# Setup of a fused four-layer graph network: edge lists loaded in other row groups and taken in another order, x in four pieces on two queues

## The chip, the core and the metric

The kernel runs on one core of one Trainium2 chip. The time is that of one execution on the device, in microseconds (us); smaller is better. A core has five engines with queues of their own: PE (TensorE, matrix products), DVE (VectorE), ACT (ScalarE), POOL (GpSimd) and SP (SyncE, which here only issues transfers). They meet through semaphores. The core's 16 DMA engines move the data.

## The reference

Four graph layers on 6,250 nodes with 128 features, 100,000 edges sorted by target, each followed by a residual sum and a layer norm:

```
x = norm(x + segsum((x @ W)[src] * (edge_attr @ edge_w), dst) + b)
x = norm(x + relu(segsum((x @ W_r)[src, edge_type] * edge_weight, dst) + bias))
x = norm(x + gcn(x, edge weights from a small MLP on x[src], x[dst]) + b)
x = norm(x + gin(x)): 4 times  h = x + segsum(x[src], dst); x = relu(h @ W1 + b1) @ W2 + b2
```

Inputs that matter here: `x` (6250 x 128, f32) and four lists of 100,000 words: `src`, `dst`, `edge_type` (integers) and `edge_weight` (f32).

## The kernel before, in words

Nodes are padded to 49 blocks of 128 (NB), handled as 7 chunks (NCH) of 7 blocks (CB). Edges are handled in 98 groups (NG) of 1024 (GE); 97 groups are full (FULL), the last holds 672 (TAIL). Each group is 8 sets (TPG) of 128 edges.

The setup, which the change rewrites, does four things side by side.

1. **Loads.** `load_list` reads a list into a tile `raw` of 98 partitions (one group in each) in two transfers: columns 0 to 671 of 98 partitions, and columns 672 to 1023 of 97 partitions. SP loads x blocks 0 to 20, dst, src, x blocks 21 to 47, and the last 106 rows of x; ACT loads W0, the types, the weights, then eight copies of `edge_w`. The second transfer of each list waits for DVE's fills (`s_fill`).
2. **Chunks.** For each chunk, `setup_turn` transposes 7 blocks of x on PE, ACT copies them out of PSUM, `setup_products` multiplies them by W0, ACT copies the product, and SP stores it to the table `xw_rows`. Before chunks 0 to 3 PE runs `turn_list`, which transposes one list each into PSUM, from where DVE takes it (`take_list`) as `srci`, `dstf`, `reli`, `wedge`.
3. **Keys and plan.** DVE waits for all eight list transfers (`s_load`), then makes three keys of each edge (`keyraw`, stored to `key_rows`) and `lists16`, then finds each group's smallest and largest target. PE turns these rows (`turn_plan`), and DVE derives `basei` and `nwini`: the plan. All engines read `nwini` (`window_count`).
4. **Histogram.** DVE marks the edges' target tiles in four wide instructions, PE sums them in two sets of 49 matmuls, and DVE forms running sums (`starts`), by which the key blocks are fetched (`c_start`).

Then comes round 0: for each of the 98 groups POOL issues 8 indirect gathers of 128 rows from `xw_rows` (line 767), PE multiplies edge attributes by `edge_w`, DVE multiplies the two (the messages, line 2091), and PE sums by target. Beside it DVE, PE and ACT build blocks of a dense matrix from the keys. POOL may run 5 groups (AHEAD) in front of the messages: the line is `pool.wait_ge(s_msg[(g - AHEAD) % 2], (g - AHEAD) // 2 + 2)`. Rounds 1 and 2 gather in the same way; the last layer uses the dense matrix. Every engine runs its instructions in program order.

On DVE `link` makes an instruction signal a semaphore and the next one wait for it. `raw` and the scratch rows `ka`, `kb` lie in `XT2`, where the gathers land, so POOL waits for `c_keys` before the first gather.

Of the kernel before, what the change touches and what calls it, by code (L numbers as in the profile page):

```python
# [6 lines left out]
I32 = mybir.dt.int32  # L7
# [34 lines left out]
def gnn_program(nc, x, src, dst, edge_attr, edge_type, edge_weight, W0, edge_w, b0, W1r, bias1,  # L42
# [28 lines left out]
    with ExitStack() as ctx:  # L71
# [205 lines left out]
        a_ready = sem2("a_ready")  # L277
        a_done = sem2("a_done")
# [22 lines left out]
        m_gath = sem2("m_gath")  # L301
        r_land = [sem(f"r_land{k}") for k in range(NS)]
# [218 lines left out]
        def _(sp):  # L521
            def x_blocks(lo, hi):
                return x[lo * P:hi * P, :].rearrange("(b p) f -> p b f", p=P)
            half = (NCH // 2) * CB
            sp.dma_start(blocks(X[:, 0:half * P]), x_blocks(0, half)).then_inc(s_xload, 16)
            for r, a in ((RDST, dst), (RSRC, src)):
                load_list(sp, r, a)
            sp.dma_start(blocks(X[:, half * P:(NB - 1) * P]), x_blocks(half, NB - 1)).then_inc(s_xload2, 16)
            sp.dma_start(X[0:LASTROWS, (NB - 1) * P:NPAD], x[(NB - 1) * P:N, :]).then_inc(s_xload2, 16)

# [71 lines left out]
            sp.wait_ge(c_list, 48)  # L602
# [142 lines left out]
        def _(pool):  # L745
            pool.iota(iota[:, :], [[1, NPAD]], base=0, channel_multiplier=0,
# [3 lines left out]
            pool.memset(acc[:, :], 0.0).then_inc(s_zero, 1)  # L750
# [21 lines left out]
            pool.wait_ge(c_keys, 1)  # L772
# [103 lines left out]
        def _(act):  # L876
            act.dma_start(W0s[:, :], W0[:, :]).then_inc(s_wload, 16)
            for r, a in ((RTYP, edge_type), (RWGT, edge_weight)):
                load_list(act, r, a)
            for j in range(TPG):  # L880
                act.dma_start(EWb[j * EDIM:(j + 1) * EDIM, j, :], edge_w[:, :]).then_inc(c_tail, 16)
# [25 lines left out]
            setup_store(NCH - 1)  # L907
            for o, i in loads:
# [390 lines left out]
        def _(pe):  # L1299
# [3 lines left out]
            def turn_list(r):  # L1303
                pe.wait_ge(s_prep, r + 1)
                if r >= 1:
                    pe.wait_ge(s_pe, r)
                v = raw[r].rearrange("g (p j) -> g j p", j=TPG)
                for j in range(TPG):
                    m = pe.transpose(ps4[:, j * P:j * P + NG], v[0:NG, j, :], ident[0:NG, 0:NG])
                m.then_inc(s_pt, 1)  # L1310

            def setup_turn(c):
                if c == 0:
                    pe.wait_ge(s_xload, 16)
                elif (c + 1) * CB > NCH // 2 * CB:
                    pe.wait_ge(s_xload2, 32)
# [17 lines left out]
            def turn_plan():  # L1334
                pe.wait_ge(s_prep, 5)
# [12 lines left out]
            pe.wait_ge(s_plan, 1)  # L1348
# [478 lines left out]
        def _(dve):  # L1827
# [8 lines left out]

            for r in (RDST, RSRC, RTYP, RWGT):
                if r == RDST:
                    dve.memset(raw[r][0:NG, TAIL:GE].bitcast(I32), -1)
                else:  # L1840
                    dve.memset(raw[r][0:NG, TAIL:GE], 0.0)
            dve.memset(X[:, (NB - 1) * P:NPAD], 0.0)
            dve.memset(EWb[:, :, :], 0.0).then_inc(s_fill, 1)
# [17 lines left out]
            dve.wait_ge(s_iota, 2)  # L1861
# [3 lines left out]
            dve.tensor_scalar(ident[:, :], iota[:, 0:P], pcol[:, 0:1], None, ALU.is_equal).then_inc(s_ident, 1)  # L1865

            dve.tensor_copy(iotaS[:, :], iota[:, 0:KS * P])
            dve.tensor_copy(iotaB[:, :], iota[:, 1:BN + 1])
            dve.wait_ge(s_ident, 1)
            dve.tensor_copy(identh[:, :], ident[:, :]).then_inc(s_ident, 1)  # L1870
            link(dve.tensor_reduce(fold[:, :], ident[:, :].rearrange("p (j c) -> p c j", c=HB), AXX, ALU.add))
            link(dve.tensor_reduce(blockof[:, :], ident[:, :].rearrange("p (j c) -> p j c", c=HB), AXX, ALU.add))


            dve.wait_ge(s_load, 16 * 8)
            lists = ((RSRC, srci), (RDST, dstf), (RTYP, reli), (RWGT, wedge))
            srcn, dstn = raw[RSRC][0:NG, :].bitcast(I32), raw[RDST][0:NG, :].bitcast(I32)
            shift_s, shift_t = (KS * P).bit_length() - 1, TB.bit_length() - 1
            link(dve.tensor_scalar(ka.bitcast(I32), srcn, KS * P - 1, None, ALU.bitwise_and))
            link(dve.tensor_copy(keyraw[:, :, 0], ka.bitcast(I32)))  # L1880
            link(dve.tensor_scalar(ka.bitcast(I32), srcn, shift_s - shift_t, 15 * TB, ALU.logical_shift_right, ALU.bitwise_and))
            link(dve.tensor_copy(kb.bitcast(I32), srcn))
            link(dve.tensor_copy(raw[RSRC][0:NG, :], srcn))
            dve.sem_inc(s_prep, 1)
            link(dve.tensor_scalar(kb.bitcast(I32), kb.bitcast(I32), P - 1, None, ALU.bitwise_and))
            link(dve.tensor_copy(lists16.rearrange("g (j p) -> g p j", p=P), kb.bitcast(I32).rearrange("g (p j) -> g p j", j=TPG)))
            link(dve.tensor_scalar(kb.bitcast(I32), dstn, TB - 1, None, ALU.bitwise_and))
            link(dve.scalar_tensor_tensor(keyraw[:, :, 1], ka.bitcast(I32), 1.0, kb.bitcast(I32), ALU.add, ALU.add))
            link(dve.tensor_scalar(ka.bitcast(I32), dstn, shift_t, None, ALU.logical_shift_right))
            link(dve.tensor_copy(keyraw[:, :, 2], ka.bitcast(I32)))  # L1890
            link(dve.tensor_copy(raw[RDST][0:NG, :], dstn))
            dve.sem_inc(s_prep, 1)

            def take_list(r):
                dve.wait_ge(s_pt, r + 1)
# [3 lines left out]

            take_list(RSRC)  # L1900
            link(dve.tensor_copy(raw[RTYP][0:NG, :], raw[RTYP][0:NG, :].bitcast(I32)))
            link(dve.scalar_tensor_tensor(raw[RTYP][0:NG, :], raw[RSRC][0:NG, :], float(RELS), raw[RTYP][0:NG, :],
                                          ALU.mult, ALU.add))
            dve.sem_inc(s_prep, 2)


            link(dve.tensor_scalar(ka, raw[RDST][0:NG, :], 0.0, float(NPAD), ALU.is_lt, ALU.mult))
            link(dve.tensor_tensor(ka, ka, raw[RDST][0:NG, :], ALU.add))
            link(dve.tensor_reduce(small[0:NG, 0:1], ka, AXX, ALU.min))
            link(dve.tensor_reduce(small[0:NG, 1:2], raw[RDST][0:NG, :], AXX, ALU.max))  # L1910
            take_list(RDST)
            link(dve.tensor_tensor(kb[:, 0:GE - P], raw[RDST][0:NG, 0:GE - P], ka[:, P:GE], ALU.is_equal))
            link(dve.tensor_reduce(small[0:NG, 2:3], kb[:, 0:GE - P], AXX, ALU.max))
# [4 lines left out]
            take_list(RTYP)  # L1918
            take_list(RWGT)

            dve.wait_ge(s_pt, 5)
# [16 lines left out]
            dve.sem_inc(c_keys, 1)  # L1938
            dve.sem_inc(s_plan, 1)
            nwin, more = window_count(dve)  # L1940

# [221 lines left out]
            dve.wait_ge(c_list, 48)  # L2163
# [434 lines left out]
```

## Time and profile before

| | us |
|---|---|
| median of 3 runs (4726.57 to 4737.44) | 4734.65 |
| the profiled execution's own time | 4725.84 |
| its span, first to last instruction | 4723.9 |
| POOL busy in the span | 2448.5 |
| PE busy in the span | 3383.4 |
| DVE busy in the span | 2343.9 |

The profile is of one execution. Its span lies 1.94 us below that execution's time, and that execution 8.8 us below the median of the runs. Line numbers in the rows are those of the kernel before. In a row `128x1024 f32` is partitions by elements; `[0.76 <-DVE big L2091]` is idle time before the instruction and what ended it. SPq, ACTq and DVEq are instructions of an engine's queue that are not counted as work, such as issuing a transfer or reading a value.

### The profile page before, as it was taken

Reading aid. Unit: us, or ns where it says so; the run is one execution under the profiler, and the core shown is the slowest. Engines: PE = TensorE matmul, PEld = TensorE weight load, DVE = VectorE, ACT = ScalarE, POOL = GpSimd, SP = SyncE. Lnnn points to the kernel's source line nnn. Section 1 sums busy time; section 2 is a strip of 40 time slices with the busy share of each in tenths; the row PEclk is TensorE's granted clock in tenths of the full one; section 3 lists DMA queues with packets and bytes.
Section 4 is the critical chain, followed back from the end, with each engine's and each line's share of the span. In section 5 each row is a group of like instructions: output and inputs, shape, how many; then the busy total and the mean of one; then the engine's idle time right before and its main releaser. Section 6 shows DMA issues by size and latency. Waiting matters only on the chain.

```text
span 4723.9 us, 66594 instructions
## 1 busy us (share of the span) xinstructions
PE 3383.4 (72%) x22549; PEld 2232.3 (47%) x22549; DVE 2343.9 (50%) x5563; ACT 1316.7 (28%) x3113; POOL 2448.5 (52%) x2489
## 2 busy tenths in 40 slices
PE   3888888886667777674333333337888999999998
PEld 3554555553445455443222222227884555555554
DVE  6755555553565556554555555556883111111122
ACT  1232322332122222222444444445882000000000
POOL 3777777774777777775777777772330000000000
PEclk8999999998888888886555555557999999999999
DMA  3334344442333333333777777777876777777776
GB/s 106 104 118 124 122 134 130 129 124 96 92 96 98 100 103 101 99 92 95 199 199 197 198 200 200 196 198 257 301 283 257 286 288 280 279 275 278 287 293 226
DMA packets 506525, 855.10 MB, mean 181 GB/s; under 512 B 111339, under 2 KB 284439, under 8 KB 506180
## 3 DMA queue, kind: packets, MB, share of 16 engines
q1 hardware_dynamic: 338752, 542.03, 32.6%
q0 software_dynamic: 87808, 179.98, 15.1%
q10 hardware_dynamic: 79620, 128.70, 7.6%
q8 instruction: 190, 3.11, 0.3%
q14 instruction: 155, 1.27, 0.1%
HBM read 632.93 MB, written 217.55 MB: 180 GB/s over the span
## 4 chain that ended last, share of the span: by engine, by line
POOL 48%; PE 30%; issue 16%; DVE 3%; DMA 1%; ACT 1%; SPq 0%; DVEq 0%; POOLq 0%; ACTq 0%
POOL big L767 32%; POOL big L794 16%; PE psS L1775 11%; PE psA L1775 11%; PE psS L1451 4%; PE psA L1655 1%; PE ps L1721 1%; PE ps L1712 1%; ACT big L1143 1%; DVE xsb L1956 1%; DMA big<-in_src_dram 0%; PE ps L1644 0%; DMA big<-A_rows 0%; PE ps L1386 0%; PE psS L1356 0%
## 5 line engine op out<-in xcount | busy, mean ns | idle before, releaser
L767 POOL DMA_INDIRECT big<-ht_rows,reli x784 | 788.4, 1006 | 276.7 <-issue 238.6
L767 POOL DMA_INDIRECT big<-xw_rows,srci x784 | 766.9, 978 | 309.5 <-issue 238.3
L794 POOL DMA_INDIRECT big<-axt_rows,srci x784 | 746.1, 952 | 264.8 <-issue 238.5
L1451 PE MATMUL psS<-big 128*128 128x128 f32 x3136 | 506.8, 329 | 311.3 <-DMA big<-ht_rows,reli 310.1
L1451 PEld LDWEIGHTS psS<-big 128*128 128x128 f32 x3136 | 475.5, 240 | 381.8 <-DMA big<-ht_rows,reli 347.6
L851 POOL TENSOR_TENSOR xsb<-xsb,l3b2r 128x896 f32<-128x896 f32 x6 | 12.5, 2079 | 1114.9 <-DMA xsb<-x_keep 1114.9
L1775 PE MATMUL psS<-big,xsb 128*128 128x448 f16 x1372 | 485.3, 354 | 17.6 <-ACT xsb L1198 15.0
L1596 PE MATMUL ps<-identh,xsb 128*128 128x128 bf16 x784 | 101.4, 311 | 549.0 <-DVE xsb L2267 549.0
L1775 PE MATMUL psA<-big,xsb 128*128 128x448 f16 x1372 | 485.1, 354 | 0.0
L1775 PE MATMUL psS<-big,acc 128*128 128x448 f16 x1372 | 483.8, 353 | 0.0
L1775 PE MATMUL psA<-big,acc 128*128 128x448 f16 x1372 | 483.8, 353 | 0.0
L929 ACT CAST xsb<-ps 128x416 f16<-128x416 f32 x392 | 197.8, 505 | 759.1 <-PE ps L1499 759.1
L1499 PE MATMUL ps<-xsb 128*128 128x416 bf16 x1960 | 401.5, 363 | 0.0
L1486 PE MATMUL psA<-xsb 128*128 128x416 bf16 x1960 | 363.1, 339 | 0.0
L1596 PEld LDWEIGHTS ps<-identh,xsb 128*128 128x128 bf16 x784 | 75.5, 141 | 577.2 <-DVE xsb L2267 577.2
L1523 PE MATMUL ps<-xsb,attrT 128*128 128x512 f32 x392 | 212.6, 669 | 127.7 <-DVE big L2091 127.3
L2033 DVE TENSOR_SCALAR xsb<-iotaS,keys 128x512 bf16<-128x512 f16 x980 | 285.2, 356 | 34.2 <-PE ps L1499 21.7
L2091 DVE TENSOR_TENSOR big<-big,ps 128x1024 f32<-128x1024 f32 x98 | 119.5, 1219 | 363.7 <-DMA big<-xw_rows,srci 363.6
L929 ACT CAST xsb<-psA 128x416 f16<-128x416 f32 x392 | 198.1, 505 | 356.8 <-PE psA L1486 356.1
L1499 PEld LDWEIGHTS ps<-xsb 128*128 128x128 bf16 x1960 | 199.4, 105 | 160.2 <-issue 39.9
L1999 DVE TENSOR_TENSOR big<-big,dstf 128x1024 f32<-128x1024 f32 x196 | 240.0, 1224 | 57.4 <-issue 36.4
L2036 DVE TENSOR_SCALAR xsb<-iotaB,kk 128x416 bf16<-128x416 f16 x980 | 263.4, 331 | 0.0
(291 smaller groups left out, 5074.1 us busy)
## 6 DMA issues: line engine op xcount, KB each, us to landing
big<-A_rows SPq DMA_DIRECT2D x112, 2744.0 KB, 13.4
A_rows<-xsb ACTq DMA_DIRECT2D x196, 416.0 KB, 2.6
xg_rows<-big SPq DMA_DIRECT2D x98, 512.0 KB, 3.8
big<-xg_rows SPq DMA_DIRECT2D x98, 512.0 KB, 4.1
marks_rows<-big SPq DMA_DIRECT2D x98, 354.0 KB
big<-marks_rows SPq DMA_DIRECT2D x98, 354.0 KB, 5.5
big<-srcq_list SPq DMA_DIRECT2D x98, 256.0 KB
ht_rows<-big ACTq DMA_DIRECT2D x28, 512.0 KB
```

Source lines behind the costliest of these rows:

```text
L767: pool.indirect_dma_start(ring[g % len(ring)][:, j * D:(j + 1) * D], None, table[:, :], bass.IndirectOffsetOnAxis(ap=lists[:, g * TPG + j: ...
L794: pool.indirect_dma_start(wide[g % NS][:, j, :], None, axt_rows[:, :], bass.IndirectOffsetOnAxis(ap=srci[:, g * TPG + j:g * TPG + j + 1], ...
L929: act.copy(Astage[:, u, :, k, :], bank(k).rearrange("p (s n) -> p s n", n=TB)).then_inc(b_ev, 1)
L1451: m = pe.matmul(psS[b][:, 0:P], rows[b][:, j * P:(j + 1) * P], marks[b][:, j * P:(j + 1) * P], start=(j == 0), stop=(j == TPG - 1))
L1486: mm = pe.matmul(bank(k), ohS[:, u, (j * KS + k) * P:(j * KS + k + 1) * P], ohB[:, u, j * BN:(j + 1) * BN], start=(j == 0), stop=(j == BT ...
L1499: mm = pe.matmul(bank(k), ohS[:, u, (j * KS + k) * P:(j * KS + k + 1) * P], ohB[:, u, j * BN:(j + 1) * BN], start=(j == 0), stop=(j == BT ...
L1523: m = pe.matmul(ps4[:, h * 512:(h + 1) * 512], attrT[:, b, :], EWb[:, 4 * h:4 * h + 4, :].rearrange("p j f -> p (j f)"), start=True, stop= ...
L1596: m = pe.transpose(turned(b)[:, j * P:(j + 1) * P], ohN[:, b, j * P:(j + 1) * P], identh[:, :])
L1775: m = pe.matmul(sums, parts_of(l, t // CB)[:, t % CB, k, :], Aring[:, r, :, t, :], start=(t == 0), stop=(t == NB - 1))
L1999: return dve.tensor_tensor(tiles(onehot[:, b, :]), iota[:, window(base, w)].unsqueeze(1).broadcast_to([P, TPG, P]), columns(dstf, it, b), ...
L2033: dve.tensor_scalar(ohS[:, u, j * KS * P:(j + 1) * KS * P], iotaS[:, :], keys[:, u, j, 0:1], None, ALU.is_equal)
L2036: last = dve.tensor_scalar(ohB[:, u, j * BN:(j + 1) * BN], iotaB[:, :], kk[:, u, j:j + 1], None, ALU.is_equal)
```

## The change

- Each list is loaded as 96 whole rows of 1024, then 2 rows of 672, then the 352 words that are left of row 96. src and dst have semaphores of their own (those of `a_ready`, whose later wait count is raised by 48).
- x is loaded in pieces of 1, 2, 2 and 2 chunks. SP issues piece 0, src, dst, and piece 2; ACT issues W0, piece 1, types, weights, piece 3 and the last 106 rows. The eight `edge_w` transfers come after the chunks.
- `raw`, `ka`, `kb` lie in `acc`; the float copies of src and dst (`srcf`, `dstc`) lie in `xsb`. POOL no longer waits for `c_keys`. ACT zeroes `acc` after the lists have been taken, where POOL did it at the start.
- POOL writes the first 128 columns of `iota` and `pcol`, and the other 6144 columns after DVE has made `ident`.
- DVE handles src and dst first, then the plan, then the types, the keys, the last two lists, and `iotaS` and `iotaB`.
- PE turns src behind the products of chunk 0, dst behind chunk 2, the plan's rows behind chunk 3, types and weights behind chunk 6.
- `key_rows` is stored as 96 rows, 1 row and 1 short row, before as 98 and 97 rows.

The diff, cut to its core:

```diff
-        raw = [XT2[:, k * GE:(k + 1) * GE] for k in range(4)]
+        raw = [acc[:, k * GE:(k + 1) * GE] for k in range(4)]
-        ka, kb = (XT2[0:NG, k * GE:(k + 1) * GE] for k in (4, 5))
+        ka, kb = (acc[0:NG, k * GE:(k + 1) * GE] for k in (4, 5))
+        srcf, dstc = (xsb[0:NG, k * GE:(k + 1) * GE] for k in range(2))
+        PIECES = ((0, 1), (1, 3), (3, 5), (5, NCH))
...
+        WHOLE = FULL - 1
+        def load_rows(eng, r, a, done):
+            v = raw[r] if r == RWGT else raw[r].bitcast(I32)
+            eng.dma_start(v[0:WHOLE, :], a[0:WHOLE * GE].rearrange("(g e) -> g e", e=GE)).then_inc(done, 16)
+            eng.dma_start(v[WHOLE:NG, 0:TAIL], bass.AP(tensor=a.tensor, offset=WHOLE * GE, ap=[[GE, NG - WHOLE], [1, TAIL]])
+                          ).then_inc(done, 16)
+        def load_rest(eng, r, a, done):
+            v = raw[r] if r == RWGT else raw[r].bitcast(I32)
+            eng.dma_start(v[WHOLE:FULL, TAIL:GE], as_row(a[WHOLE * GE + TAIL:FULL * GE])).then_inc(done, 16)
+        def load_x(eng, k):
+            lo, hi = PIECES[k][0] * CB, min(PIECES[k][1] * CB, NB - 1)
+            eng.dma_start(blocks(X[:, lo * P:hi * P]), x[lo * P:hi * P, :].rearrange("(b p) f -> p b f", p=P)
+                          ).then_inc(x_in[k], 16)
...
+            load_x(sp, 0)
+            load_rows(sp, RSRC, src, s_lsrc)
+            load_rows(sp, RDST, dst, s_ldst)
+            sp.wait_ge(s_fill, 1)
+            load_rest(sp, RSRC, src, s_lsrc)
+            load_rest(sp, RDST, dst, s_ldst)
+            load_x(sp, 2)
...
             pool.wait_ge(s_plan, 1)
-            pool.wait_ge(c_keys, 1)
...
             act.dma_start(W0s[:, :], W0[:, :]).then_inc(s_wload, 16)
+            load_x(act, 1)
             for r, a in ((RTYP, edge_type), (RWGT, edge_weight)):
-                load_list(act, r, a)
-            for j in range(TPG):
-                act.dma_start(EWb[j * EDIM:(j + 1) * EDIM, j, :], edge_w[:, :]).then_inc(c_tail, 16)
+                load_rows(act, r, a, s_load)
+            load_x(act, 3)
+            act.wait_ge(s_fill, 1)
+            act.dma_start(X[0:LASTROWS, (NB - 1) * P:NPAD], x[(NB - 1) * P:N, :]).then_inc(x_in[3], 16)
+            for r, a in ((RTYP, edge_type), (RWGT, edge_weight)):
+                load_rest(act, r, a, s_load)
...
+            act.wait_ge(s_iota, 3)
+            act.wait_ge(s_pe, 4)
+            act.activation(acc[:, :], iota[:, :], ACT.Copy, scale=0.0).then_inc(s_zero, 1)
...
             for c in range(NCH):
-                if c < 4:
-                    turn_list(c)
-                elif c == 4:
-                    turn_plan()
                 if c + 1 < NCH:
                     setup_turn(c + 1)
                 setup_products(c)
+                if c == 0:
+                    turn_list(RSRC)
+                elif c == 2:
+                    turn_list(RDST)
+                elif c == 3:
+                    turn_plan()
+            turn_list(RTYP)
+            turn_list(RWGT)
```

How the order moves on two engines. On PE, the first matmuls of the setup before (`psA<-ident,big` are `setup_turn`, `ps<-ident,big` a list, `ps<-W0s` the products):

```order
L1320 MATMUL psA<-ident,big 128x128 x7
L1309 MATMUL ps<-ident,big 128x98 x8
L1320 MATMUL psA<-ident,big 128x128 x7
L1330 MATMUL ps<-W0s,xTs 128x128 x7
L1309 MATMUL ps<-ident,big 128x98 x8
L1320 MATMUL psA<-ident,big 128x128 x7
L1330 MATMUL ps<-W0s,xn 128x128 x7
```

and of the change, where the lists lie in `xsb` (src, dst) and `acc`:

```order
L1349 MATMUL psA<-ident,big 128x128 x14
L1359 MATMUL ps<-W0s,xTs 128x128 x7
L1339 MATMUL ps<-ident,xsb 128x98 x8
L1349 MATMUL psA<-ident,big 128x128 x7
L1359 MATMUL ps<-W0s,xn 128x128 x7
L1349 MATMUL psA<-ident,big 128x128 x7
L1359 MATMUL ps<-W0s,xTs 128x128 x7
L1339 MATMUL ps<-ident,xsb 128x98 x8
```

The first list now stands behind two turned chunks and the first products; the plan's three rows stand behind chunk 3 here, and stood behind all four lists before.

On DVE, from the last step on a list's smallest and largest values to the plan, before:

```order
L1915 TENSOR_REDUCE small<-big 98x1
L1916 TENSOR_TENSOR small<-small 98x1
L1896 CAST reli<-ps 128x8x98
L1896 COPY wedge<-ps 128x8x98
L1923 COPY rowf<-psS 1x98
L1924 TENSOR_TENSOR rowf<-psS,rowf 1x98
```

and, in the change, from the end of the plan to the histogram's first instruction (types, keys, `lists16`, two lists taken, `iotaS`, `iotaB`):

```order
L1954 CAST acc<-acc 98x1024
L1955 SCALAR_TENSOR_TENSOR acc<-xsb,acc 98x1024
L1957 TENSOR_SCALAR acc<-acc 98x1024
L1958 CAST big<-acc 98x1024
L1959 TENSOR_SCALAR acc<-acc 98x1024
L1960 TENSOR_SCALAR acc<-acc 98x1024
L1961 SCALAR_TENSOR_TENSOR big<-acc 98x1024
L1962 TENSOR_SCALAR acc<-acc 98x1024
L1963 CAST big<-acc 98x1024
L1964 TENSOR_SCALAR acc<-acc 98x1024
L1965 CAST xsb<-acc 98x128x8
L1915 CAST reli<-ps 128x8x98
```

The first of the change's rows comes right behind DVE's reading of `nwini`; behind the last stand `wedge`, `iotaS` and `iotaB`, then the copy into `psS` with which the histogram begins (line 1946 before). Before, all this work but the histogram stood ahead of the plan.

## Rows read from the trace of the kernel before

**Rows 1.** Page, part 5, the gathers of the first round (line 767)

```profile
L767 POOL DMA_INDIRECT big<-xw_rows,srci x784 | 766.9, 978 | 309.5 <-issue 238.3
```

**Rows 2.** Waits of POOL: total us, times, longest us

```profile
POOL big L767 <- DMA xw_rows<-big: 70.4, 1, 70.4
...
POOL big L767 <- DVE big L2091: 0.8, 1, 0.8
```

**Rows 3.** Chain that ended last, first 140 us: start, us, what

```profile
12.03 22.27 DMA big<-in_src_dram
34.39 0.70 DVE big L1879
...
45.49 0.70 DVE big L1891
...
67.34 0.26 DVE rowf L1923
...
73.42 0.19 DVE psS L1946
...
123.76 2.90 issue
...
131.37 1.14 DVE big L2091
...
132.76 1.68 POOL big L767
```

**Rows 4.** Timeline of SP's and ACT's queues: start us, us, issue

```profile
9.59 15.40 ACTq L881 DMA_DIRECT2D xsb<-in_L_gnn_edge_w_dram  x8
...
24.31 11.76 SPq L529 DMA_DIRECT2D big<-in_x_dram  x1
25.33 1.28 ACT L889 ACT_TABLE_LOAD   x1 [25.33 <-issue]
26.63 0.91 ACT L889 COPY xTs<-psA 128x896 f32<-128x896 f32 x1
```

**Rows 5.** Windows: each engine's busy us, PEclk, DMA share, GB/s

```profile
4.00:8.00 4.00, 0.00 (x0) 0.00 (x0) 2.73 (x17) 0.00 (x0) 4.00 (x3) 1.00 1.05 291
15.00:20.00 5.00, 0.00 (x0) 0.00 (x0) 0.00 (x0) 0.00 (x0) 0.00 (x0) 1.00 0.07 25
```

**Rows 6.** Timeline of TensorE, setup matmuls at the slow and fast rate

```profile
56.82 1.55 PE L1309 MATMUL ps<-ident,big 98*128 98x98 f32 x8 [3.82 <-DVEq L1898]
...
58.16 1.70 PE L1320 MATMUL psA<-ident,big 128*128 128x128 f32 x7
...
59.66 2.82 PE L1330 MATMUL ps<-W0s,xTs 128*128 128x128 f32 x14
...
68.14 1.80 PE L1330 MATMUL ps<-W0s,xTs 128*128 128x128 f32 x14
...
71.02 1.80 PE L1330 MATMUL ps<-W0s,xn 128*128 128x128 f32 x14 [0.32 <-ACT big L895]
```

**Rows 7.** Timeline of DVE in the setup, one memset of POOL

```profile
6.23 5.31 POOL L750 MEMSET acc<- 128x6272 f32 x1
...
6.55 5.35 DVE L1867 CAST iotaS<-big 128x512 f16<-128x512 f32 x1
...
11.82 0.36 DVE L1868 CAST iotaB<-big 128x416 f16<-128x416 f32 x1
...
46.33 1.56 DVE L1896 CAST srci<-ps 128x784 int32<-128x784 f32 x1 [0.15 <-DVE big L1891]
...
48.45 0.69 DVE L1901 CAST big<-big 98x1024 f32<-98x1024 int32 x1 [0.56 <-DVE srci L1896]
...
50.56 0.69 DVE L1907 TENSOR_SCALAR big<-big 98x1024 f32<-98x1024 f32 x1 [0.16 <-DVE big L1902]
```

**Rows 8.** Timeline, the first gather, then DVE's markings in the loop

```profile
81.93 1.14 POOL L767 DMA_INDIRECT big<-xw_rows,srci  x1 [70.39 <-DMA xw_rows<-big]
...
128.75 1.40 DVE L2033 TENSOR_SCALAR xsb<-iotaS,keys 128x512 bf16<-128x512 f16 x5
```

More of the change, by code:

```diff
@@ L277, in gnn_program @@
         a_ready = sem2("a_ready")
+        s_lsrc, s_ldst = a_ready
+        LISTED = 16 * 3
         a_done = sem2("a_done")
@@ L301, in gnn_program @@
         m_gath = sem2("m_gath")
+        x_in = [s_xload, *m_gath, s_xload2]
+        PIECED = 16
         r_land = [sem(f"r_land{k}") for k in range(NS)]
@@ L521, in _ @@
         def _(sp):
[L522 to L529, printed above, removed]
+            load_x(sp, 0)
[5 more added lines that the diff above has]
+            load_x(sp, 2)
             def rows_of(table, c):
@@ L745, in _ @@
         def _(pool):
-            pool.iota(iota[:, :], [[1, NPAD]], base=0, channel_multiplier=0,
+            pool.iota(iota[:, 0:P], [[1, P]], base=0, channel_multiplier=0,
                       allow_small_or_imprecise_dtypes=True).then_inc(s_iota, 1)
@@ L749, in _ @@
                       allow_small_or_imprecise_dtypes=True).then_inc(s_iota, 1)
-            pool.memset(acc[:, :], 0.0).then_inc(s_zero, 1)
+            pool.wait_ge(s_ident, 1)
+            pool.iota(iota[:, P:], [[1, NPAD - P]], base=P, channel_multiplier=0,
+                      allow_small_or_imprecise_dtypes=True).then_inc(s_iota, 1)
             def gathers(it, idx_ready, gathered, table):
@@ L907, in _ @@
             setup_store(NCH - 1)
+            act.wait_ge(s_fill, 2)
+            for j in range(TPG):
+                act.dma_start(EWb[j * EDIM:(j + 1) * EDIM, j, :], edge_w[:, :]).then_inc(c_tail, 16)
             for o, i in loads:
@@ L1312, in setup_turn @@
             def setup_turn(c):
[L1313 to L1316, printed above, removed]
+                for k, (lo, hi) in enumerate(PIECES):
+                    if c == lo:
+                        pe.wait_ge(x_in[k], 2 * PIECED if hi == NCH else PIECED)
                 if c:
@@ L1834, in link @@
                 dve.wait_ge(s_chain, chain[0])
+            dve.wait_ge(s_iota, 2)
+            dve.tensor_scalar(ident[:, :], iota[:, 0:P], pcol[:, 0:1], None, ALU.is_equal).then_inc(s_ident, 1)
             for r in (RDST, RSRC, RTYP, RWGT):
                 if r == RDST:
-                    dve.memset(raw[r][0:NG, TAIL:GE].bitcast(I32), -1)
+                    dve.memset(raw[r][WHOLE:NG, TAIL:GE].bitcast(I32), -1)
                 else:
-                    dve.memset(raw[r][0:NG, TAIL:GE], 0.0)
-            dve.memset(X[:, (NB - 1) * P:NPAD], 0.0)
-            dve.memset(EWb[:, :, :], 0.0).then_inc(s_fill, 1)
+                    dve.memset(raw[r][WHOLE:NG, TAIL:GE], 0.0)
+            dve.memset(X[:, (NB - 1) * P:NPAD], 0.0).then_inc(s_fill, 1)
+            dve.wait_ge(s_ident, 1)
+            dve.tensor_copy(identh[:, :], ident[:, :]).then_inc(s_ident, 1)
+            link(dve.tensor_reduce(fold[:, :], ident[:, :].rearrange("p (j c) -> p c j", c=HB), AXX, ALU.add))
+            link(dve.tensor_reduce(blockof[:, :], ident[:, :].rearrange("p (j c) -> p j c", c=HB), AXX, ALU.add))
+            dve.memset(EWb[:, :, :], 0.0)
             dve.memset(attr[:, :, :], 0.0)
@@ L1864, in _ @@
             dve.memset(invs[:, 0, 1:2], 1.0 / (FIRST * LOW))
[L1865 to L1871, printed above, removed]
@@ L1887, in _ @@
[L1887 to L1891, printed above, removed]
+            dve.wait_ge(s_lsrc, LISTED)
+            link(dve.tensor_copy(srcf, srcn))
@@ L1898, in take_list @@
                 dve.sem_inc(s_pe, 1)
-            take_list(RSRC)
[L1901 to L1913, printed above, removed]
+            link(dve.tensor_scalar(ka, dstc, 0.0, float(NPAD), ALU.is_lt, ALU.mult))
+            link(dve.tensor_tensor(ka, ka, dstc, ALU.add))
+            link(dve.tensor_reduce(small[0:NG, 0:1], ka, AXX, ALU.min))
+            link(dve.tensor_reduce(small[0:NG, 1:2], dstc, AXX, ALU.max))
+            link(dve.tensor_tensor(kb[:, 0:GE - P], dstc[:, 0:GE - P], ka[:, P:GE], ALU.is_equal))
+            link(dve.tensor_reduce(small[0:NG, 2:3], kb[:, 0:GE - P], AXX, ALU.max))
+            take_list(RSRC)
             link(dve.tensor_tensor(kb[:, 0:GE - 1], ka[:, 0:GE - 1], ka[:, 1:GE], ALU.is_gt))
@@ L1917, in _ @@
             dve.sem_inc(s_prep, 1)
-            take_list(RTYP)
-            take_list(RWGT)
-            dve.wait_ge(s_pt, 5)
+            take_list(RDST)
+            dve.wait_ge(s_pt, 3)
             lo, hi, span, base = (rowf[:, k, :] for k in range(4))
@@ L1937, in _ @@
             link(dve.tensor_copy(nwini[:, :], hi[:, 2:4]))
-            dve.sem_inc(c_keys, 1)
             dve.sem_inc(s_plan, 1)
             nwin, more = window_count(dve)
+            shift_s, shift_t = (KS * P).bit_length() - 1, TB.bit_length() - 1
+            dve.wait_ge(s_load, 16 * 6)
+            link(dve.tensor_copy(raw[RTYP][0:NG, :], raw[RTYP][0:NG, :].bitcast(I32)))
+            link(dve.scalar_tensor_tensor(raw[RTYP][0:NG, :], srcf, float(RELS), raw[RTYP][0:NG, :], ALU.mult, ALU.add))
+            dve.sem_inc(s_prep, 2)
+            link(dve.tensor_scalar(ka.bitcast(I32), srcn, KS * P - 1, None, ALU.bitwise_and))
+            link(dve.tensor_copy(keyraw[:, :, 0], ka.bitcast(I32)))
+            link(dve.tensor_scalar(ka.bitcast(I32), srcn, shift_s - shift_t, 15 * TB, ALU.logical_shift_right, ALU.bitwise_and))
+            link(dve.tensor_scalar(kb.bitcast(I32), dstn, TB - 1, None, ALU.bitwise_and))
+            link(dve.scalar_tensor_tensor(keyraw[:, :, 1], ka.bitcast(I32), 1.0, kb.bitcast(I32), ALU.add, ALU.add))
+            link(dve.tensor_scalar(ka.bitcast(I32), dstn, shift_t, None, ALU.logical_shift_right))
+            link(dve.tensor_copy(keyraw[:, :, 2], ka.bitcast(I32)))
+            link(dve.tensor_scalar(kb.bitcast(I32), srcn, P - 1, None, ALU.bitwise_and))
+            link(dve.tensor_copy(lists16.rearrange("g (j p) -> g p j", p=P), kb.bitcast(I32).rearrange("g (p j) -> g p j", j=TPG)))
+            dve.sem_inc(c_keys, 1)
+            take_list(RTYP)
+            take_list(RWGT)
+            dve.wait_ge(s_iota, 3)
+            dve.tensor_copy(iotaS[:, :], iota[:, 0:KS * P])
+            dve.tensor_copy(iotaB[:, :], iota[:, 1:BN + 1])
             HSH = HB.bit_length() - 1
```

38 lines of the change are left out of this document (13 added, 25 removed).

## The prediction

> **What bounds the kernel now.** I read the page first, then POOL's waits, the chain that ended last over the first 140 us, and the timelines of each engine there. In the page the 784 gathers of round 0 are 767 us of POOL work plus 310 us of idle time between them, most of it issue [rows 1]: POOL paces that round, so what moves POOL's steady stream moves all that follows. POOL's stream could begin when the table `xw_rows` is stored; it waited 70.4 us for it [rows 2] and began at 81.93 [rows 8]. But it may run only 5 groups, 40 gathers, in front of DVE's messages. The 41st gather began at 132.76 [rows 3], and POOL had waited 0.8 us for DVE's first message [rows 2], which ran at 131.37. So at this place the two sides are nearly level: an earlier first gather alone gives at most 0.8 us, and an earlier DVE gives nothing unless the first gather moves too. The change moves both.
>
> The chain of waits says what sets DVE: src lands at 34.30 (12.03 + 22.27), DVE starts on the keys at 34.39, reaches the plan at 67.34, the histogram at 73.42 and the loop after 123.76 [rows 3]. From 73.42 on nothing is edited on DVE, and I carry that stretch over as it is. The question is thus: at which time does DVE begin the histogram?
>
> The loads explain the 34.30. From 4 to 8 us the DMA engines moved 291 GB/s; from 15 to 20 us they moved 25 GB/s at a share of 0.07, about one engine of 16 [rows 5]. Meanwhile the queues stood: ACT was busy until 24.99 issuing eight small transfers, and SP until 36.07 with the last issue of x [rows 4]. I read the 25 GB/s as the 97-row transfers, 97 rows of 1408 bytes each: four of them are 0.546 MB, and at 25 GB/s 21.9 us, which fits the gap.
>
> **The change part by part.** *Loads.* Now the bulk is 96 whole rows a list. x is 3.2 MB, the lists 1.6 MB, W0 0.07 MB: 4.87 MB at 291 GB/s are 16.7 us, from about 2 us on, so all has landed by about 19 us. src and dst stand ahead of half of x on SP; with the two queues taking turns they land near 12 us. I estimate that ACT's last issue ends at 17.5 us: a transfer's issue seems to end a little ahead of the data before it. Bounds: 12 us if ACT's queue gets the larger share, 19 us if the smaller. The last 106 rows of x still go as a transfer of their own, in that ACT queue.
> By the Trainium skill ("DMA: Bandwidth & Descriptors", section on why a DMA increments its semaphore by 16) a transfer uses the largest number of engines up to 16 that divides its rows: one for 97, all for 96, but two for 106. Taking the row's 25 GB/s for an engine, 54 KB on two is 1.1 us, which would put the sum 1.1 us later; the trace agrees for 97 rows.
>
> *First copy of ACT.* Behind its last issue ACT loads its table and copies chunk 0 out: from 24.99 to 27.54, 2.55 us [rows 4]. So now 20.1 us. `ident` is made before POOL's long iota and not after, but was ready at 11.7 us already: worth nothing by itself.
>
> *PE up to the plan.* Slow matmuls: list 1.55, turned chunk 1.70, products 2.82 [rows 6], together 6.1: 26.2. At the fast rate a chunk takes 2.88 (68.14 to 71.02) [rows 6]. Before, PE came up after about 6 us of unbroken work; I take chunk 1 half way, 3.8, then 2.9 with a list of 1.1 for chunk 2, 2.9 for chunk 3, and 0.6 for the plan's rows: 26.2 + 3.8 + 4.0 + 2.9 + 0.6 = 37.5. DVE has its side ready long before: from 12 us two casts (0.7 each), 0.7, and five wide steps near 1.2 take it to about 20; it takes src at 26.3 and ends at 30.7. So the plan begins on DVE at 37.5, before at 67.34.
>
> *DVE from the plan to the histogram.* Plan and reading of `nwini`: 67.34 to 73.42, 6.08 us [rows 3], unchanged. Behind it now comes what stood ahead of it: types, 48.45 to 50.56, 2.11 [rows 7]; keys and `lists16`: 34.39 to 45.49 is 11.10 [rows 3], less the copy to `kb` that is gone and the cast of src that is now earlier, 0.70 each like the first row, 1.57 with their gaps and signals, so 9.53; two takes of 1.56 [rows 7] with gaps 1.6 each; one list on PE between them, 1.65 with its signals, at the slow rate since PE stands still then; `iotaS` and `iotaB` 0.9, from 0.36 for 416 columns [rows 7]. Sum: 6.08 + 2.11 + 9.53 + 1.6 + 1.65 + 1.6 + 0.9 = 23.5, and 37.5 + 23.5 = 61.0. Before it was 73.42. **The histogram starts 12.4 us earlier.**
>
> *What is free.* PE ends its chunks and the types at about 47, DVE takes them at 55. The last products are out at about 45; ACT's copy, the store and its landing are some 6 us, an estimate, so the last of `xw_rows` is in at about 51, the first gather goes out then, so group 4 ends at about 101 (50 us before, 81.93 to 132); DVE's first message falls at 131.37 - 12.4 = 119.0: POOL waits some 18 us, where it waited 0.8, and that is cover for anything that is late on the x side, up to 18 us. ACT zeroes `acc` from 60, by its copy of 0.91 for 896 columns [rows 4] 6.4 us, ended by 67, needed after 111. `edge_w` and weights, issued from 46, are needed near 108. POOL's iota of 6144 columns, 5.2 us by its memset [rows 7], may hold DVE's early fills until 8 us, but the lists land at 12. The keys are stored from 55 on, needed after 111. The new order of `key_rows` shortens a transfer that nothing waits for.
>
> *Total.* POOL's 41st gather goes out at 132.76 - 12.4 = 120.4, and all behind it shifts. The profiled execution of 4725.84 would become 4713.4; against the median of the runs, 4734.65 - 12.4 = 4722.3 us, 0.26% less. About 0.2%, 9.5 us, is what a measurement of this kernel can tell from no change.
>
> **The rivals.**
> *PE stays slow in the setup.* Then a chunk takes 4.7 (1.70 + 2.82 + gaps) instead of 2.9: 0.9 more for chunk 1, 2.2 for chunk 2 with its list, 1.8 for chunk 3. The plan comes 4.9 later, the gain is 7.5: 4727.2. For it: between 38 and 56 us PE worked at slow durations through three chunks; against it: it had pauses of 4 us there [rows 6], which now go.
> *DVE and POOL hinder each other.* The gathers now start at 51, while DVE still has about five copies and masks of the keys and two casts from `iota` to do. Before, `iotaS` took 5.35 us beside POOL's memset of 5.31 [rows 7], 15 times `iotaB`. If each of five waits up to one gather, 0.94 us, the gain falls by 4.7 to 7.7: 4727.0. Against it: beside the gathers of the loop DVE's five markings took 1.40 us, 0.28 each [rows 8], while POOL's gather there stretched to 1.68 [rows 3]; POOL waits, not DVE, and POOL has 18 us to spare.
> The Trainium skill ("SBUF — State Buffer", section on two separate sides) has the two share a port pair as an exclusive lock, held for the whole instruction; that is this rival, and the row of `iotaS` agrees with it, the markings do not show DVE paying.
> *The first gather decides.* If my reading of the 5-group limit were wrong, the gain would be 81.93 - 51 = 31: 4704. The wait for DVE's message speaks against it.
> *The loads still crawl (slower).* The mechanism: ACT issues 27 of 48 blocks of x and has to copy every chunk; if its last issue ends as late as SP's did, 36.07 [rows 4], the first copy is at 38.6, 18.5 later than in my sum, the histogram starts at 79.5 instead of 73.42: 6.1 us slower, 4740.8. It decides from 29.9 us on, 17.5 + 12.4. This would take another transfer that runs on one engine for over 10 us; I see none of that size.
>
> **How the numbers follow.** Forecast 0.61; PE slow 0.18; DVE and POOL 0.07; first gather 0.03; loads crawl 0.06; the rest, 0.05, is an ACT queue done at 12 us, gain 17.9: 4716.8. Faster by over 0.2%: nearly all of the first (0.57), the first gather and the early queue 0.08, a little of PE slow: 0.66. Slower: a part of the crawling loads and of what I don't see, 0.06. Same: 0.28. Range for 8 in 10: from the early queue with 2 us of scatter, 4715, to a PE that stays slow together with a queue 5 us late, 4732.
>
> **What would show it.** DMA near 290 GB/s from 3 to 18 us without the stretch at 0.07; ACT's first copy near 20; the plan's first DVE row near 37.5; the copy into `psS` that begins the histogram near 61; the first gather near 51, a wait of POOL for DVE's message near 18 us, and the 41st gather near 120. The prediction is wrong if ACT's first copy comes after 25, if PE's chunks stay at 4.7 us, or if DVE's 50.3 us from histogram to loop grow because gathers run beside all of it.

## The result

The changed kernel took 4714.92 us in the median of 5 runs (4713.01 to 4722.19), the kernel before 4733.25 in 5 runs of the same chip. The ratio is 0.9963 with a 95% interval of 0.9952 to 0.9975: 17.5 us less, between 11.8 and 22.7. Forecast were 12.4 us. The profiled execution took 4713.99 us with a span of 4711.6.

The chain that ended last in the changed kernel, first 135 us (start, us, what):

```profile
17.23 0.27 ACTq L527
17.84 1.28 ACT L913
19.13 0.92 ACT xTs L913
...
33.75 0.26 DVE rowf L1934
...
106.11 2.94 issue
...
113.73 1.14 DVE big L2122
```

It answers to [rows 3]. DVE's plan starts at 33.75 (before 67.34), the stretch behind the histogram ends at 106.1 (before 123.8), and ahead of the plan the chain now runs through ACT's queue and its first copy, not through a landing list. DVE's rows in the timeline (the figure ahead of the engine is the duration; a wait and what ended it stand in brackets): the cast of src as it lands, the take of the turned src behind the wait for PE, the last step on the keys, the histogram's first row and the first message:

```profile
10.39 0.69 DVE L1907 CAST xsb<-acc 98x1024 f32<-98x1024 int32 x1
...
25.17 1.58 DVE L1915 CAST srci<-ps 128x784 int32<-128x784 f32 x1 [6.39 <-PE ps L1339]
...
48.97 2.45 DVE L1965 CAST xsb<-acc 98x1024 bf16<-98x1024 int32 x1
...
57.23 0.17 DVE L1977 COPY psS<-big 128x16 f32<-128x16 f32 x1
...
113.64 1.22 DVE L2122 TENSOR_TENSOR big<-big,ps 128x1024 f32<-128x1024 f32 x1
```

DVE has src at 10.4 us (before 34.39), waits 6.39 us for PE to turn it, and begins the histogram at 57.23 (before 73.42). POOL's timeline and waits:

```profile
46.41 1.14 POOL L788 DMA_INDIRECT big<-xw_rows,srci  x1 [39.62 <-DMA xw_rows<-big]
...
115.13 3.62 POOL L788 DMA_INDIRECT big<-xw_rows,srci  x1 [16.91 <-DVE big L2122]
119.06 0.94 POOL L788 DMA_INDIRECT big<-xw_rows,srci  x1 [0.30 <-issue]
```

```profile
POOL big L788 <- DMA xw_rows<-big: 39.6, 1, 39.6
...
POOL big L788 <- DVE big L2122: 17.2, 2, 16.9
```

They answer to [rows 2] and [rows 8]. The first gather goes out at 46.41 and not at 81.93, 35.5 us earlier, but the 41st only 17.6 earlier (115.13 against 132.76), since it waits 16.9 us for the first message. That single row is the cover that the prediction put at 18 us. It runs 3.62 us, where the same gather ran 1.68 in the kernel before.

The DMA engines while the lists and x come in (last two columns: share, GB/s), to be held against [rows 5], and ACT's queue against [rows 4]:

```profile
2.00:5.00 3.00, 0.00 (x0) 0.00 (x0) 2.88 (x6) 0.00 (x0) 3.00 (x1) 1.00 0.98 286
...
15.00:20.00 5.00, 0.00 (x0) 0.00 (x0) 3.68 (x4) 2.15 (x2) 0.00 (x0) 1.00 1.05 255
20.00:25.00 5.00, 4.82 (x30) 4.85 (x31) 0.00 (x0) 1.72 (x3) 0.00 (x0) 1.00 0.03 9
```

```profile
6.47 6.22 ACTq L903 DMA_DIRECT2D big<-in_x_dram  x1
...
12.73 4.47 ACTq L527 DMA_DIRECT2D acc<-in_edge_type_dram  x1
...
17.84 1.28 ACT L913 ACT_TABLE_LOAD   x1 [17.84 <-issue]
```

From 15 to 20 us the engines are nearly full where they stood at 0.07, and all is in by about 20 us.

### The profile page after: what moved, and what is told of

The parts are those of the page before. It is cut to its first block, busy times and chain, and to the rows that moved or that the text cites. A ratio compares the mean times of both kernels' runs of the same rounds, so it can differ in the third digit from the quotient of the medians.

```text
span 4711.6 us, 66597 instructions
## 1 busy us (share of the span) xinstructions
PE 3379.1 (72%) x22549; PEld 2229.9 (47%) x22549; DVE 2347.8 (50%) x5562; ACT 1323.1 (28%) x3114; POOL 2442.7 (52%) x2489
## 4 chain that ended last, share of the span: by engine, by line
POOL 47%; PE 31%; issue 16%; DVE 3%; ACT 1%; DMA 1%; ACTq 0%; DVEq 0%; POOLq 0%; SPq 0%
POOL big L788 32%; POOL big L814 16%; PE psS L1808 11%; PE psA L1808 11%; PE psS L1484 4%; PE psA L1688 1%; PE ps L1754 1%; PE ps L1745 1%; ACT big L1173 1%; DVE xsb L1987 1%; PE ps L1677 0%; DMA big<-A_rows 0%; PE psA L1519 0%; PE ps L1419 0%; PE psS L1389 0%
## 5 line engine op out<-in xcount | busy, mean ns | idle before, releaser
L1532 PEld LDWEIGHTS ps<-xsb 128*128 128x128 bf16 x1960 | 200.1, 106 | 160.8 <-issue 41.4
```

The source lines that it names most:

```text
L1532: mm = pe.matmul(bank(k), ohS[:, u, (j * KS + k) * P:(j * KS + k + 1) * P], ohB[:, u, j * BN:(j + 1) * BN], start=(j == 0), stop=(j == BT ...
```

## The experiments

Each kernel was measured together with the kernel before on the same chip (three chips in all), so ratios to the kernel before are what compares across them; the changed kernel's is 0.9963 (0.9952 to 0.9975). Two ratios 0.0015 apart still have overlapping intervals. There I add the start of the last gather of round 0 from the profiles, one execution each: 1087.0 us before, 1071.0 in the changed kernel.

**The old row groups put back.** The changed kernel with 98 rows of 672 words and 97 rows of 352 for each list:

```diff
-            eng.dma_start(v[0:WHOLE, :], a[0:WHOLE * GE].rearrange("(g e) -> g e", e=GE)).then_inc(done, 16)
-            eng.dma_start(v[WHOLE:NG, 0:TAIL], bass.AP(tensor=a.tensor, offset=WHOLE * GE, ap=[[GE, NG - WHOLE], [1, TAIL]])
-                          ).then_inc(done, 16)
+            eng.dma_start(v[0:NG, 0:TAIL], bass.AP(tensor=a.tensor, offset=0, ap=[[GE, NG], [1, TAIL]])).then_inc(done, 16)
...
-            eng.dma_start(v[WHOLE:FULL, TAIL:GE], as_row(a[WHOLE * GE + TAIL:FULL * GE])).then_inc(done, 16)
+            eng.dma_start(v[0:FULL, TAIL:GE], a[0:FULL * GE].rearrange("(g e) -> g e", e=GE)[:, TAIL:GE]).then_inc(done, 16)
```

> The changed kernel with the old row groups of the lists (98 rows of 672 words, 97 rows of 352 words) and all else as changed. Theory A (the 97-row transfers run on one DMA engine, and that is what held the loads before): the stretch at about 25 GB/s comes back for 10 to 20 us, the last issue of ACT ends near 30 us and not near 17.5, the histogram on DVE starts at 68 to 74 us and not at 57.2, and the time is within 5 us of the kernel before, some 4728 to 4736. Rival B (the gain is the new order of the work and the two queues for x, not the rows): ACT's last issue stays below 22 us, the histogram below 61, and the time near 4716.

Measured: 4718.15 us against 4725.56, ratio 0.9984 (0.9975 to 0.9993). Its windows (share, GB/s last), two casts of DVE on src and dst, and ACT's table load, which follows its last issue:

```profile
23.00:35.00 12.00, 5.94 (x34) 5.97 (x35) 7.47 (x8) 4.00 (x4) 0.00 (x0) 1.00 0.07 24
```

```profile
18.18 0.69 DVE L1905 CAST xsb<-acc 98x1024 f32<-98x1024 int32 x1 [7.90 <-DMA acc<-in_src_dram]
26.03 0.69 DVE L1908 CAST xsb<-acc 98x1024 f32<-98x1024 int32 x1 [7.17 <-DMA acc<-in_dst_dram]
...
68.12 0.17 DVE L1975 COPY psS<-big 128x16 f32<-128x16 f32 x1
```

```profile
19.85 6.52 ACTq L525 DMA_DIRECT2D acc<-in_edge_weight_dram  x1
26.72 1.28 ACT L911 ACT_TABLE_LOAD   x1 [26.72 <-issue]
```

The crawl at 24 GB/s is back for 12 us, dst comes 14.8 us later than in the changed kernel, and the histogram starts at 68.12, 10.9 later. Theory A stands and B falls. But 7.5 us of gain are left, where A had at most 5: in the new order DVE's first step waits for src alone and began at 18.18, before at 34.39. The 12 us at 24 GB/s are 0.29 MB, about two of the 97-row transfers of 0.137 MB. This kernel has the 98-row transfers back as well; what these cost by themselves was not run, and the share of 0.07 (one engine of 16) is what points at the 97-row ones.

**The row groups alone.** The kernel before with the list loads of the change, nothing else:

```diff
-            eng.dma_start(v[0:NG, 0:TAIL], bass.AP(tensor=a.tensor, offset=0, ap=[[GE, NG], [1, TAIL]])).then_inc(s_load, 16)
+            eng.dma_start(v[0:WHOLE, :], a[0:WHOLE * GE].rearrange("(g e) -> g e", e=GE)).then_inc(s_load, 16)
+            eng.dma_start(v[WHOLE:NG, 0:TAIL], bass.AP(tensor=a.tensor, offset=WHOLE * GE, ap=[[GE, NG - WHOLE], [1, TAIL]])
+                          ).then_inc(s_load, 16)
             eng.wait_ge(s_fill, 1)
-            eng.dma_start(v[0:FULL, TAIL:GE], a[0:FULL * GE].rearrange("(g e) -> g e", e=GE)[:, TAIL:GE]).then_inc(s_load, 16)
+            eng.dma_start(v[WHOLE:FULL, TAIL:GE], as_row(a[WHOLE * GE + TAIL:FULL * GE])).then_inc(s_load, 16)
```

> The kernel before with only the list loads (and the fills) cut as in the change: 96 whole rows, 2 rows of 672, 1 row of 352. Order of the work, tiles and queues stay. Theory A: all lists are in near 13 to 16 us instead of 34.3, so DVE's chain of 39 us to the histogram starts about 20 us earlier and the histogram at 52 to 56 us: the gain is at least that of the whole change, 4711 to 4716. Rival B: DVE then waits for PE's and ACT's chunks, the histogram starts after 60 and the gain is half of the change's or less, 4724 or more.

Measured: 4708.44 against 4725.56, ratio 0.9962 (0.9949 to 0.9975): all of the change's gain, and below the 4711 to 4716 that were expected. DVE's first step on the keys, and the histogram's start, in the timeline:

```profile
16.76 0.69 DVE L1882 TENSOR_SCALAR big<-big 98x1024 int32<-98x1024 int32 x1 [3.85 <-DMA big<-in_src_dram]
...
55.78 0.18 DVE L1949 COPY psS<-big 128x16 f32<-128x16 f32 x1 [2.40 <-issue]
```

```profile
64.40 1.14 POOL L770 DMA_INDIRECT big<-xw_rows,srci  x1 [52.86 <-DMA xw_rows<-big]
```

The histogram starts 17.6 us earlier than before, even 1.4 us earlier than in the changed kernel, and the first gather 17.5 us earlier. With both sides moved alike, POOL has no wait for the message, and the last gather of round 0 goes out at 1066.9 us, 4 us ahead of the changed kernel's. So, at a lead of 5, the new order of the work, the four pieces of x and the move of the lists added nothing that can be measured here.

**The first gather 13 us late.** The changed kernel with one wait more:

```diff
             pool.wait_ge(s_plan, 1)
+            pool.wait_ge(s_pe, 4)
```

> The changed kernel, in which POOL also waits until all four lists have been taken, so the first gather goes out near 57 us and not at 46.4. Theory D (DVE's first message decides, POOL has 16.9 us to spare): the 41st gather stays at 115 us, POOL's wait for DVE's message shrinks from 16.9 to about 6, and the time stays at 4715, within 3 us. Rival G (the first gather decides): 10 us more, 4725.

Measured: 4712.56 against 4725.56, ratio 0.9964 (0.9950 to 0.9977). The first gather is at 59.59 us and not 46.41, the 41st here:

```profile
116.08 3.62 POOL L788 DMA_INDIRECT big<-xw_rows,srci  x1 [6.52 <-DVE big L2123]
```

The wait shrank from 16.9 to 6.5 and the time did not move: D holds, G falls. This kernel also speaks on the rival in which DVE and POOL hinder each other: with no gathers beside them, DVE's steps from the plan to the histogram took 23.36 us (34.41 to 57.77), with gathers 23.48 (33.75 to 57.23).

**Lead of 7 groups, and of 6.** One number of the changed kernel:

```diff
-AHEAD = 5
+AHEAD = 7
```

> The changed kernel with POOL allowed 7 groups in front of the messages instead of 5 (AHEAD 7; there are 7 slots). Theory D: POOL's wait of 16.9 us before the 41st gather is gone, the 57th gather can go out at about 116.5 just after the first message at 114.9, and the whole stream is 17 to 20 us earlier: 4695 to 4699. Rival: something else (DVE's catching up, PE, the transfers) holds round 0 then, and the end of the round moves by less than 5 us: 4710 or more.

> The changed kernel with a lead of 6 groups. Theory D: the 49th gather could go out at about 107 us and waits until the first message at 114.9, so a wait of 8 us stays of the 16.9; the time lies halfway between lead 5 and lead 7, about 10 us above the latter's (ratio 0.9946). Rival: lead 5 to 7 gained by something else than this first wait, and 6 is like 7.

Lead 7: 4692.93 against 4725.56, ratio 0.9926 (0.9913 to 0.9939). Lead 6: 4699.06 against 4725.21, ratio 0.9946 (0.9932 to 0.9959). POOL's waits with lead 7, where the row for DVE's message is gone, and with lead 6:

```profile
POOL big L788 <- DMA xw_rows<-big: 40.5, 1, 40.5
```

```profile
POOL big L788 <- DMA xw_rows<-big: 40.5, 1, 40.5
...
POOL big L788 <- DVE big L2122: 8.2, 2, 7.9
```

A wait of 16.9, 7.9 and none gives 17.5, 25.5 and 35.0 us of gain (1 less the ratio, times 4725). The intervals of leads 5 and 6, and of 6 and 7, overlap; those of 5 and 7 do not. The last gather of round 0 goes the same way: 1071.0, 1062.2 and 1056.7. This is the same wait, paid out step by step.

**The row groups alone, with lead 7.** The kernel of the second experiment and `AHEAD = 7`:

> The kernel before with the new row groups of the lists and a lead of 7 groups, order of the work as before. Theory: the new order of the work gave nothing at a lead of 5 (rows alone had the whole gain) since it moves the first gather, from about 64 to 46 us, which has slack there; at a lead of 7 it is the first gather that decides, so this kernel gains no more than 2 us over the rows alone (ratio 0.996) and stays 14 to 18 us behind the changed kernel with the lead of 7 (0.9926). Rival: the order is worth nothing in any case, ratio near 0.993 here too.

Measured: 4705.37 against 4725.08, ratio 0.9955 (0.9942 to 0.9969), 13.7 us behind the changed kernel with lead 7. Its first gather is at 64.38 us, 17 us later than there (47.3). In the profiles the last gather of round 0 is 8.9 us later than there (1065.6 against 1056.7), and most of what comes on top lies in round 1, which took 1031.1 us from its first to its last gather here and 1020 to 1027 in the other profiles. So the new order is worth 9 to 14 us, but only where the lead lets the first gather count.

**Keys in DVE's gap.** The changed kernel with the nine instructions of the keys ahead of the first plan step:

```diff
+            link(dve.tensor_scalar(ka.bitcast(I32), srcn, KS * P - 1, None, ALU.bitwise_and))
+            link(dve.tensor_copy(keyraw[:, :, 0], ka.bitcast(I32)))
...
+            dve.sem_inc(c_keys, 1)
             link(dve.tensor_scalar(ka, dstc, 0.0, float(NPAD), ALU.is_lt, ALU.mult))
```

> The changed kernel with the keys (9.5 us of DVE work) moved ahead of the plan's steps, into the stretch in which DVE waits 6.4 us for PE to turn src. Theory D: plan and first gather stay where they are (33.8 and 46.4 us), the histogram starts at 49 to 51 us instead of 57.2, POOL's wait for the message shrinks from 16.9 to 9 to 11 us, and the time is 6 to 8 us below the changed kernel. Rival G (first gather decides): no change in time.

Measured: 4699.42 against 4725.08, ratio 0.9950 (0.9936 to 0.9964). The histogram starts at 50.01 us, the 41st gather goes out at 109.36 behind a wait of 11.6, and the last gather of round 0 at 1064.0, 7.0 us ahead of the changed kernel's. The ratio gives 6 us, as expected, but the intervals overlap, so it is the profile that shows the gain. The plan (35.12 us) and the first gather (47.9) were even some 1.4 us later than in the changed kernel: DVE's side decides.

**All of x on SP's queue**, with lead 5 and with lead 7:

```diff
             load_rest(sp, RDST, dst, s_ldst)
+            load_x(sp, 1)
             load_x(sp, 2)
+            load_x(sp, 3)
+            sp.dma_start(X[0:LASTROWS, (NB - 1) * P:NPAD], x[(NB - 1) * P:N, :]).then_inc(x_in[3], 16)
...
-            load_x(act, 1)
...
-            load_x(act, 3)
             act.wait_ge(s_fill, 1)
-            act.dma_start(X[0:LASTROWS, (NB - 1) * P:NPAD], x[(NB - 1) * P:N, :]).then_inc(x_in[3], 16)
```

> The changed kernel with all pieces of x on SP's queue behind the lists, ACT issues W0, types and weights alone (lead of POOL 5, as changed). Theory Q (the plan waits for ACT, whose queue is held by issues until 17.5 us): ACT's first copy falls from 19.1 to 7 to 9 us, the plan on DVE from 33.75 to about 26, the histogram from 57.2 to 49 to 51, the first gather from 46.4 to about 39, and the time is 6 to 8 us below that of the changed kernel. Rival: x's later pieces, now behind one another on one queue, hold the chunks, plan and first gather stay within 2 us, and so does the time.

> The changed kernel with all x on SP's queue and a lead of 7 groups. Theory D with both: the first gather decides now; it moves from 46.4 to about 39 us, the 57th to 109, just behind the first message at 107, and the time is 6 to 8 us below the kernel with the lead of 7 alone, whose ratio to the kernel before was 0.9926: ratio 0.991. Rival: DVE's first message comes later than 109 and takes up the difference; ratio 0.9926.

Lead 5: 4700.77 against 4725.08, ratio 0.9948 (0.9935 to 0.9962). Lead 7: 4690.21 against 4725.08, ratio 0.9921 (0.9907 to 0.9935). PE's turning of chunks 0 and 1 with lead 5, and the plan's first row on DVE:

```profile
15.20 1.76 PE L1349 MATMUL psA<-ident,big 128*128 128x128 f32 x7 [8.58 <-DMA big<-in_x_dram]
16.75 2.38 PE L1359 MATMUL ps<-W0s,xTs 128*128 128x128 f32 x14
```

```profile
28.69 0.25 DVE L1934 COPY rowf<-psS 1x98 f32<-1x98 f32 x1 [0.98 <-PE psS L1367]
...
52.20 0.17 DVE L1977 COPY psS<-big 128x16 f32<-128x16 f32 x1
```

ACT's first copy is at 6.65 us and not 19.13, but now PE waits for x until 15.2. The plan comes at 28.7, 5 us earlier and not 8; the histogram (52.2) and the first gather (41.4) come 1 to 2.5 us after their expected times. The gain over the changed kernel is 7 us with lead 5, with overlapping intervals; the last gather of round 0 is 6.2 us earlier (1064.8). With lead 7 the first gather is 5.2 us earlier (42.1 against 47.3), and so is the last gather of round 0 (1051.2 against 1056.7), but the ratio moves by 0.0005 only, inside the intervals: the 6 to 8 us that were expected are not shown in the time.

**Types and weights behind x.** The last kernel, lead 7, with `load_rows` and `load_rest` of the types and weights taken from ACT to the end of SP's loads:

> The kernel with all x on SP's queue and a lead of 7 groups, and the types and weights moved from ACT's queue to the end of SP's, behind x. Theory: there the turning of chunk 1 on PE waits until 15.2 us for x, which shares the DMA engines with the types and weights that nothing needs before 30 us; now it starts at 10 to 12 us, the plan on DVE moves from 29.5 to 25 to 27 and the first gather from 42.1 to 37 to 39 us, and the time is 3 to 5 us (0.1%) below that kernel's. Rival: the plan waits for DVE's own steps on src and dst (to about 24 us) and the first gather moves by less than 2 us.

Measured: 4686.49 against 4725.21, ratio 0.9910 (0.9894 to 0.9925). PE turns chunk 1 at 11.18 us, the plan is at 26.32, the first gather at 38.93, all as expected. The last step in time, 0.9921 to 0.9910, is inside the intervals; against the changed kernel, 0.9963, it is not. This is the fastest version of the study: 0.9% below the kernel before.

## Why the prediction held, point by point

- **The number.** The forecast gain was 12.4 us, the measured one 17.5, and the median of 4714.92 lies at the lower end of the range (4715; the range was counted from 4734.65 for the kernel before, which here had 4733.25). That is the size of the last rival, an ACT queue done at 12 us (17.9), but by another way: ACT's queue ended at 17.5, as in the sum. The histogram started 16.2 us early, 12.4 of the forecast and 3.7 from PE up to the plan; with 1.5 behind the histogram this gives the 17.6 of the 41st gather. Both terms are below.
- **The bound.** Both readings held: POOL's stream follows from DVE's first message at a lead of 5 (late gather, leads 6 and 7), and the first gather has slack there.
- **The loads.** Right in mechanism and size. ACT's last issue ended at 17.5 us, as estimated; DVE took src at 10.4 without a wait, and not at 12. The old row groups are what held them, shown by putting them back and by changing them alone. That it was the 97-row transfers rests on their bytes and the share of 0.07.
- **PE up to the plan.** Mis-sized. The sum had 17.4 us from ACT's first copy to the plan, the trace 13.7 (20.04 to 33.75). The term at fault is the slow rate: I let it last through chunk 0, its list and half of chunk 1. PE's rows:

```profile
20.18 1.73 PE L1349 MATMUL psA<-ident,big 128*128 128x128 f32 x7 [13.42 <-ACT xTs L913]
...
21.70 2.49 PE L1359 MATMUL ps<-W0s,xTs 128*128 128x128 f32 x14
...
24.03 1.03 PE L1339 MATMUL ps<-ident,xsb 98*128 98x98 f32 x8
...
24.89 0.93 PE L1349 MATMUL psA<-ident,big 128*128 128x128 f32 x7
```

The products of chunk 0 took 2.49 instead of 2.82, and the list behind them 1.03 instead of 1.55: the list at 24.03, 3.9 us after PE began at 20.18, already ran at the fast duration, where the sum let the slow one last for some 6 us. With chunk 1 all fast as well, that is 2.2 of the 3.7 us. The rest is in the chunks: the sum had 2.9 for each fast one, but from the start of the turned blocks to the start of what follows the products, chunks 1 and 3 took 2.3 (24.89 to 27.22, 30.97 to 33.30), since there the products began 0.77 us after the turned blocks; in the chunk of 2.9 it was 1.25 us, with a wait of 0.32 for ACT's copy [rows 6].

That PE's slow stretch can be shorter stood in the trace of the kernel before. The prediction says that PE worked at slow durations through three chunks, and took its time from the third. In the first two, the products were nearly at the fast 1.80 (granted clock 1.00 from 41.0 to 43.1 us, against 0.61 from 59.6 to 62.6 in the third):

```profile
41.13 1.88 PE L1330 MATMUL ps<-W0s,xTs 128*128 128x128 f32 x14
...
50.88 2.12 PE L1330 MATMUL ps<-W0s,xn 128*128 128x128 f32 x14
```

In the variants with the same order on PE these products took from 2.38 to 3.20 us, so about 1 us of this term differs from one execution to the next. The granted clock does not tell when it turned: from 20 to 34 us it reads 1.00 in the changed kernel, the higher of its two levels, also while the matmuls were slow.
- **DVE from the plan to the histogram.** 23.5 forecast, 23.48 measured.
- **Histogram to first message.** Carried over at 57.9 us, measured 56.4 (57.23 to 113.64). The two sets of 49 matmuls on PE took 4.78 and 4.17 us, before 5.42 and 4.81. That is 1.3 of the 1.5 us. The granted clock over them was 0.59 and 0.68, before 0.50 and 0.59; why it was higher is open.
- **What is free.** First gather 46.4 (51 forecast): the last products ended at 42.1 and not 45, and copy, store and landing took 4.3 and not 6. Wait 16.9 (18 forecast), 41st gather 115.1 (120.4 forecast).
- **From there to the end.** The 41st gather was 17.6 us early, the 42nd 15.7 (119.06 against 134.75), the last of round 0 16.0, the last gather of round 2 15.2, the end of the span 12.3. The stretch behind that last gather lay between 1525.6 and 1531.5 us in the twelve profiles of this kernel and its variants, in no order that follows the edits, so the 3 us lost there in one profile are scatter. The runs' ratio, 17.5, fits the 16 us at the end of round 0.
- **What the prediction did not see.** It booked the gain to the whole change: the plan 30 us earlier, 17.5 us of work moved behind it. With the new row groups alone the plan is at 49.69 us. Against that, the new order brings it forward by 16 us (33.75) and puts the 17.5 us of work behind it: on DVE these two nearly cancel, and what is left is the arrival of the lists. At a lead of 5 the new row groups, alone, give the whole gain. The parts do not add up, though: on top of the new order the row groups are worth 10 us (0.9984 to 0.9963).
- **The rivals.** A PE that stays slow and the loads that crawl did not come; DVE and POOL hindering each other cost 0.1 us on DVE; the first gather did not decide at a lead of 5, and does at 7. Of the single-engine worry for the last 106 rows, ACT's queue shows issues of 6.22 and 4.47 us, the 6.22 being that of these rows, but x was all in at 20 us. With all of x on SP's queue ACT's issues took 0.6 us at most, and the issue of the 106 rows took 2.90 us on SP, behind 10.7 us for three pieces of x. So the long issues go with the queue that carries x; what in it they wait for is open.

## What to carry to other kernels

Look in the first microseconds for a stretch in which the DMA share is one engine's (here 0.07) and transfers are pending: here it went with four transfers of 97 rows, and loading 96 whole rows in their place was worth 17 us by itself. Where a producer may run a fixed number of groups ahead, moving its start only pays up to the point where that lead is used up; read the wait at the end of the lead before and after, and raise the lead if there are free slots. And make the smallest version of a change as well: here it had all the gain, and the rest of the change became worth something only with one more number changed.

## What the runs showed of the hardware that was not expected

The first gather after POOL's long wait for DVE's message took 3.62 us (in six kernels: 115.13 in the changed one, and those with the old rows, the late gather, lead 6, keys in the gap and x on SP), where most gathers take 0.94 and the same gather of the kernel before took 1.68. In all six it starts 0.35 us into a wide multiplication of DVE (114.77 in the changed kernel) and ends 0.1 us behind the last of the ten short markings that follow (118.63). Here this gives back 1.9 of the 17.6 us. Why it lasts through the markings is open: in the kernel before, the gather at 132.76 starts at the same place of DVE's steps and took 1.68.

DVE's cast of `identh` took 3.64 us beside POOL's long iota, for 0.21 before:

```profile
1.54 5.25 POOL L770 IOTA big<- 128x6144 f32 x1 [0.39 <-DVE ident L1871]
...
3.23 3.64 DVE L1879 CAST identh<-ident 128x128 bf16<-128x128 f32 x1
```

It ended at 6.87, when the iota had ended at 6.79, and cost nothing, since DVE later waited 6.39 us for PE. In the Trainium skill ("SBUF — State Buffer", section on two separate sides) this is one port pair held for a whole instruction by either engine; the rows agree for this cast.
